# A fused attention, memory and expert kernel: tiles of scores for the row maxima are issued ahead of the turns, projections and products with the values of their tick

## The reference

```python
x = x + xattn(layernorm(x), ctx, ctx)     # 16 query heads of 32, one key/value head, 2048 keys, softmax
x = x + attn(layernorm(x))                # gated linear memory, 4 heads of 128, chunks of 64
x = x + ffn(layernorm(x))                 # 16 experts, the best one per token, 512 -> 2048 -> 512, capacity 128
```

## Time and profile before

| what | value |
|---|---|
| median of 3 runs (lowest to highest) | 2172.67 us (2171.48 to 2175.91) |
| profiled execution, its own time | 2173.11 us |
| its span, first to last instruction | 2171.3 us |
| mean granted clock of PE | 0.986 of full |
| PE busy | 2095.7 us, 97% |
| PEld busy | 1421.6 us, 65% |
| POOL / DVE / ACT busy | 75% / 59% / 56% |

### The profile page before, as it was taken

The page is one execution under the profiler, slowest core; times in us unless marked ns, Lnnn a source line. Parts: engine busy times, 40 slices in busy tenths (PEclk is TensorE's granted clock), DMA queues, the critical chain, the costliest instruction groups (busy, mean ns, idle before and its releaser), DMA issues. The chain is left out here.

```text
span 2171.3 us, 35745 instructions
## 1 busy us (share of the span) xinstructions
PE 2095.7 (97%) x12908; PEld 1421.6 (65%) x12908; DVE 1272.3 (59%) x2226; ACT 1220.7 (56%) x2277; POOL 1635.7 (75%) x1387
## 2 busy tenths in 40 slices
PE   7879999999999999999999999999989999999999
PEld 5436565656565656666565656565645789999998
DVE  5656767676666666676767676766664433333332
ACT  3756575666666566666665666666655233433333
POOL 0778888888888888888888888889798145555555
PEclk8989999999999999999999999999999999999999
DMA  4752121212212121212131212112200089999994
GB/s 159 242 113 90 48 74 45 73 52 66 75 48 74 45 73 53 74 44 82 39 97 43 74 43 74 59 57 71 79 15 11 12 313 357 363 352 359 360 348 177
DMA packets 107055, 262.31 MB, mean 121 GB/s; under 512 B 8960, under 2 KB 34304, under 8 KB 98688
## 3 DMA queue, kind: packets, MB, share of 16 engines
q1 hardware_dynamic: 96912, 234.92, 31.6%
q10 hardware_dynamic: 6384, 14.62, 2.3%
q0 software_dynamic: 3584, 10.49, 1.2%
HBM read 223.67 MB, written 25.72 MB: 115 GB/s over the span
## 5 line engine op out<-in xcount | busy, mean ns | idle before, releaser
L1094 POOL TENSOR_TENSOR psum<-psum,weights 128x512 f32<-128x512 f32 x896 | 1152.6, 1286 | 163.4 <-ACT weights L702 60.5
L880 DVE TENSOR_REDUCE mpart<-bank 128x1 f32<-128x512 f32 x1024 | 680.4, 684 | 308.9 <-PE bank L447 300.0
L702 ACT ACTIVATE weights<-bank 128x512 f32<-128x512 f32 x1024 | 597.0, 599 | 324.1 <-PE bank L460 313.3
L460 PE MATMUL bank<-qT,kT 97*128 97x512 f32 x1024 | 482.8, 477 | 10.0 <-DMA qT<-mrow 6.5
L447 PE MATMUL bank<-kT,qT 96*128 96x512 f32 x1024 | 450.0, 451 | 9.6 <-DVE mpart L880 6.8
L447 PEld LDWEIGHTS bank<-kT,qT 96*128 96x128 f32 x1024 | 196.9, 192 | 141.2 <-issue 87.4
L1346 POOL TENSOR_TENSOR w2l<-w,w2h 128x1024 fp32r<-128x1024 f32 x64 | 202.9, 3171 | 75.8 <-PE ebank L1259 54.5
L460 PEld LDWEIGHTS bank<-qT,kT 97*128 97x128 f32 x1024 | 195.7, 193 | 89.4 <-issue 49.2
L472 PE MATMUL bank<-weights,v 128*32 128x512 f32 x2048 | 251.3, 609 | 0.0
L737 ACT COPY w_first<-bank 128x512 f32<-128x512 f32 x248 | 144.7, 584 | 67.6 <-PE bank L412 64.6
L1289 ACT ACTIVATE hh<-ebank 128x512 fp32r<-128x512 f32 x64 | 38.2, 597 | 224.6 <-PE ebank L1243 224.6
(11 more groups left out here) (174 smaller groups left out, 3019.3 us busy)
## 6 DMA issues: line engine op xcount, KB each, us to landing
w<-in_w SPq DMA_DIRECT2D x48, 2048.0 KB, 19.9
w_first<-in_ctx SPq DMA_DIRECT2D x62, 1024.0 KB, 5.2
w_first<-in_w SPq DMA_DIRECT2D x16, 2048.0 KB, 12.2
dispatched<-route ACTq DMA_DIRECT2D x17, 513.0 KB, 8.5
dis<-dispatched SPq DMA_DIRECT2D x16, 513.0 KB, 3.5
qT<-qh SPq DMA_DIRECT2D x128, 64.0 KB, 3.4
qT<-qs SPq DMA_DIRECT2D x64, 64.0 KB, 2.1
xr<-in_x SPq DMA_DIRECT2D x16, 256.0 KB, 2.7
```

The source lines that it names most:

```text
L460: e.matmul(B_BANK[u % 2][:], kT[b % 2][0:3 * HD + 1, k * P:(k + 1) * P], qT[b % 2][0:3 * HD + 1, g * 512:(g + 1) * 512], start=True, stop= ...
L702: e.activation(p[n % NP], B_BANK[u % 2][:], ACT.Exp).then_inc(p_act.sem, 1)
L880: e.tensor_reduce(mpart[g % 2][:, 4 * (n % 4) + n // 4:4 * (n % 4) + n // 4 + 1], max_bank(b, g, n)[:], AX.X, ALU.max).then_inc(max_dve.se ...
L1094: e.tensor_tensor(acc[:], first, p[(UNITS * b + u) % NP], ALU.add).then_inc(psum_pool.sem, 1)
```

## The change

In passes 0 to 15 PE's loop issues the tiles for the maxima directly behind the score of the tick (or first, where an odd tick has no score), in front of the preparation, the products with the values and the sums. In the passes before 0 the order stays. The lists of the other engines, the tables of ticks, all waits and all buffers stay as they are.

```diff
@@ PE's loop over passes and ticks
                 for t in range(TICKS if i <= B else TAIL):
                     if 0 <= i < B and t % 2 == 0:
                         score(i, t // 2)
+                    if i >= 0:
+                        for b, g, n in maxima_in(i, t):
+                            largest(b, g, n)
                     if i == -1 and t in WARM:
                         for _ in range(WARM[t]):
                             e.matmul(P_BANK[:, 0:P], mneg[:], mneg[:], start=True, stop=True)
...
                         weigh(b, u)
                     if 1 <= i <= B and t == POST["sums"]:
                         sums(i - 1)
-                    for b, g, n in maxima_in(i, t):
-                        largest(b, g, n)
+                    if i < 0:
+                        for b, g, n in maxima_in(i, t):
+                            largest(b, g, n)
                     for b, g in turns_in(i, t):
                         turn_max(b, g)
                     if i >= 2:
```

## The result

The changed kernel takes 2195.86 us (median of 4 runs, 2192.61 to 2200.7) against 2172.07 us for the kernel before (4 runs): ratio 1.011, 95% interval 1.0095 to 1.0125. Slower was forecast, but by 10 us, and it is 24. The time lies outside the range of 2174 to 2189.

What follows compares the result with a forecast made beforehand. PE's instruction list was taken as the length of a pass. A full pass at +0.69 us, 13 times, plus +0.45 for other passes gave +9.4 us, so 2182 us was predicted, range 2174 to 2189.

Steps and rivals of the forecast that it cites:

- tick 60: Turn 0.24 us later, its next turn three ticks or more behind; grouped with ticks 24, 26, 32, 35, 58: 0.
- tick 17: Tile ahead of the products with the values stops for DVE's reduction of tile 11; +0.41 us a full pass.
- tick 9: Tile 9 waits for DVE's reduction, so the turn starts later and tick 12's turn waits for ACT's copy; +0.34 us.
- tick 81: Tile between second-layer products and products with the values saves part of a 0.18 us extra; 0.10 us gain taken.
- Tick 13: Tile no longer fills the wait between the turns of ticks 13 and 15; +0.29 us a full pass.
- Ticks 49 and 81: Cheaper neighbours around products: a turn follows them in one, a tile parts them in the other; together -0.15 us.
- The turn of the maxima: Tick 113's tile 13 is reduced earlier, so the turn in tick 119 starts sooner; -0.20 us a full pass.
- The other passes: Pass 1 +0.35 us, pass 15 about -0.1, pass 0 +0.2 (0 to 0.4); together +0.45 us.
- B: Rival: the wait for the maxima in tick 119 goes, full pass -0.31 us, 2169 us; 8%.
- C: Rival: later waits in the pass take back PE's stops of ticks 9 to 17, about 2174 us; 12%.
- D: Rival: new stops in ticks 13 to 17 bring the clock down once a pass, 26 us more, 2209 us; 5%.
- The rule of the Trainium skill on neighbouring scores: Weight loads overlap only on other array rows: 0.19 us per new neighbouring pair, 2.9 us in all; left out.

Runs made afterwards that it cites:

- only_49_113: Kernel before with the tile moved ahead of the products with the values in ticks 49 and 113 alone; full pass 102.16 us, ratio 0.9995.
- not_9_13_17: The changed kernel without the moves of ticks 9, 13 and 17; full pass 102.34 us, ratio 0.9984.
- before_recip: Kernel before with only the first two reciprocals later in DVE's list (ticks 12, 13 instead of 10, 12); full pass 102.43 us, ratio 0.9999.
- after_recip: The changed kernel with the first two reciprocals later in DVE's list (ticks 12, 13 instead of 10, 12); full pass 103.09 us, ratio 1.0047.
- later_turn: `only_49_113` with the turn of tick 15 put in tick 16 on all engines; full pass 101.95 us, ratio 0.9983.

## Why the prediction was wrong

**Which step failed.** A full pass was forecast at +0.69 and costs +1.36. The step that failed is the pricing of the stops: I took the cost of a tile that doesn't wait for one that does, let the higher price behind the products go with the tile, and put the delay of tick 60 at nothing. The terms are tick 17 (+0.41, and it was 0.63), tick 60 (0, and it was 0.21), tick 9 (+0.34, and it was 0.51) and tick 81 (-0.10, and it was 0).

**The order of events was right in ticks 9 to 17, the sizes were too small.** Tick 9: predicted +0.34, measured +0.50 alone and 0.51 in the whole change (tile 8 to `sums` is 2.88 us there, 886.32 to 889.20, and 2.37 before, 872.53 to 874.90). A tile that has stood still costs PE 0.34 us to the next start (887.00 to 887.34), not the 0.24 that I took; and the turn of tick 12, which now waits itself, is followed by `sums` 0.59 later, not 0.53. My upper bound, 0.43, was below what it costs.

Tick 13: +0.29 predicted, +0.31 alone. Right, but not a price of its own beside tick 17, whose stop ends by DVE's clock. I had the number in the text, the reduction's end at 880.14, and didn't see that it makes tick 17 alone dearer (0.93) and tick 13 beside it free. This didn't harm the sum: the three ticks were worked out as one stretch (+1.03), and only its division among the ticks was wrong.

Tick 17: +0.41 predicted, +0.63 as what is left for it of the stretch. This is the term that failed most. Two parts: the stopped tile costs 0.43 to the start of the products (894.15 to 894.58), not 0.32. And "behind them the tile's 0.34 falls away" is wrong: the first score behind products with 32 columns pays this price whoever it is. In the changed kernel it is the score of tick 18, 896.44 to 896.78; only 0.24 fell away. These two, 0.11 and 0.10, with the 0.17 of tick 9 that `sums` and so DVE's list pass on, are the 0.38 us between the 1.04 forecast for the stretch and its 1.42.

**Ticks 24 to 60: 0 predicted, +0.21 measured, all of it tick 60.** I looked for the next turn and found it far off. I didn't follow the turn's copy through ACT's list, where two copies for the keys stand behind it, with DVE and PE behind them. My bounds had it at the very edge (+0.2).

**Ticks 49 and 81: -0.15 predicted.** In tick 81 the trace of after has the same sum as before; what the products of the second layer saved was paid at the tile, which costs 0.41 us behind them and 0.32 elsewhere, and at the score behind the products with the values. Tick 49's -0.05 held: the score of tick 50 comes 0.05 us sooner in `only_49_113` and `not_9_13_17`, counted from the score ahead of tick 49.

**The turn of the maxima: -0.20 predicted, -0.22 measured.** From tile 14 to the turn it took 2.27 us before and takes 2.05 now (979.99 to 982.04), PE in pass 8:

```profile
979.65 0.50 PE L460 MATMUL bank<-qT,kT 97*128 97x512 f32 x1
979.99 0.40 PE L447 MATMUL bank<-kT,qT 96*128 96x512 f32 x1
...
982.04 0.33 PE L452 MATMUL bank<-cst,mneg 128*128 128x128 f32 x1 [0.71 <-DVE mneg L891]
```

The reason held as well: DVE takes two reductions at once during the products and two behind them, in place of one and three:

```profile
978.94 1.28 DVE L884 TENSOR_REDUCE mpart<-bank 128x1 f32<-128x512 f32 x2
980.42 1.29 DVE L884 TENSOR_REDUCE mpart<-bank 128x1 f32<-128x512 f32 x2 [0.20 <-PE bank L447]
```

**The other passes.** Pass 1: +0.35 predicted, +0.84 measured (103.95 to 104.79), which fits the error in tick 17 plus tick 60; but pass 1 in the old order took 103.48 and 104.13 us in two other profiles, so the size is good to some 0.3 us. Pass 0: +0.2 predicted, somewhere from 1 to 5 by the runs; I looked for stops there and not at the clock, which stays low for longer. How much of the cost is the clock stays open. Pass 15: from its first score to the experts it takes 163.9 us in the kernel before and 166.8 in `before_recip`, both in the old order, and 166.7 in the changed kernel, so its part stays open.

**The sum.** 13 x 1.36 = 17.7 and pass 1 0.8 are 18.5 us; the ratio's interval gives 20.6 to 27.2 for the whole. The 5 us between 18.5 and the medians' 23.8 are pass 0 and what lies in pass 15 and in the noise of four runs, and can't be divided further.

**The rivals.** B and C fell: 0.71 of the wait at the turn is still there, and nothing gave the losses back. D fell for the full passes, whose granted clock stayed at 1.00. In pass 0, where the clock is low for a while in any case, the move of tick 9 keeps it low for longer, which neither D nor my term for pass 0 had. The rule of the Trainium skill on neighbouring scores ("TensorE: Matmul & The Clock Gate", Part 3, The mechanism) would have brought the forecast to 2185; two neighbouring tiles in `after_recip`, 0.56 us with the start of the products included, leave no room for it (887.79 to 888.35, that is 0.24 and 0.32). The same section of the Trainium skill has a second case, which I left out: a load also goes ahead of running matmuls where it targets the background weight buffer. The trace fits that case, though no row names a buffer: in the kernel after, the load of the tile of tick 16 starts at 893.16, within the score of 893.08 on the same rows. The range failed because each term's bounds were taken by the same rows as the term, and because I let errors of different ticks cancel: four of them had one sign (0.17, 0.22, 0.21 and 0.10 too low).

## What to carry to other kernels

In this kernel, work of an in-order engine that stood between an instruction and the one whose wait it covered was free (a tile in tick 13, a score in `later_turn`); moved out of that gap, it cost its full time, and a tile that was moved ahead of its release became a stop with everything behind it. Before moving an instruction forward, look in the list of the engine that releases it at what stands ahead of that release, and follow what is pushed back through the lists of all engines that read it, not only to its next peer. Prices of several moves that end in one stop don't add; here tests of each alone and of a pair showed it.

## What the runs showed of the hardware

A matmul of scores (96 rows, 512 columns) costs 0.24 us to the start of the next matmul where it stands behind another of its kind, and 0.34 where a wait has stopped it (887.00 to 887.34); ahead of products with 32 columns the two are 0.32 and 0.43 (894.15 to 894.58). I had expected a wait to cost the waiting time alone. The wait is not the only way to this price: the first score behind products with 32 columns pays 0.34 without having been stopped (880.99 to 881.33), and a score behind a turn 0.32 (887.69 to 888.01 in the kernel after).

What the dear ones share is where the record of their weights' load lies. Here are the loads of the tiles of ticks 16 and 17 in the kernel after, the second of them stopped:

```profile
893.16 0.19 PEld L447 LDWEIGHTS bank<-kT,qT 96*128 96x128 f32 x1
...
894.15 0.19 PEld L447 LDWEIGHTS bank<-kT,qT 96*128 96x128 f32 x1 [0.80 <-DVE mpart L884]
```

The first starts 0.24 us ahead of its matmul (893.40), the second together with it (894.15); behind products with 32 columns the load also starts with its matmul (880.99 in the kernel before), and behind a turn 0.02 us ahead of it (887.67). So in the dear cases the 0.19 us of the load don't lie ahead of the matmul. That the load makes the extra 0.1 us is an inference: no run changed the load alone.
